# Own attention of the last block: values as the stationary operand, probabilities streaming, sums and inverses rearranged

## The reference, cut to what matters

```
def mha(xq, ctx, wq, wk, wv, wo, bo):
    ...
    scores = jnp.einsum('bhqd,bhkd->bhqk', q, k) / math.sqrt(DH)
    attn = jax.nn.softmax(scores, axis=-1)
    out = jnp.einsum('bhqk,bhkd->bhqd', attn, v)
    out = out.transpose(0, 2, 1, 3).reshape(b, sq, INNER)
    return out @ wo + bo
h1 = adaln(x, t, norm1_w, norm1_b)
x = mha(h1, h1, attn1_wq, ...) + x      # own attention: 256 queries, 256 keys
h2 = adaln(x, t, norm2_w, norm2_b)
x = mha(h2, context, attn2_wq, ...) + x # cross attention: 64 keys
h3 = adaln(x, t, norm3_w, norm3_b)
x = glu_ff(h3, ff_w1, ff_b1, ff_w2, ff_b2) + x
```

## Time and profile before

| | us |
|---|---|
| median of 3 runs | 5301.52 (5294.6 to 5302.85) |
| the profiled execution, its own time | 5300.39 |
| its span in the trace | 5298.2 |
| TensorE busy | 4622.3 (87% of the span) |
| VectorE / ScalarE / GpSimd busy | 2879.5 / 2086.8 / 574.2 |

### The profile page before, as it was taken

The page is one execution under the profiler, slowest core; times in us unless marked ns, Lnnn a source line. Parts: engine busy times, 40 slices in busy tenths (PEclk is TensorE's granted clock), DMA queues, the critical chain, the costliest instruction groups (busy, mean ns, idle before and its releaser), DMA issues. The chain is left out here.

```text
span 5298.2 us, 111277 instructions
## 1 busy us (share of the span) xinstructions
PE 4622.3 (87%) x45501; PEld 3101.2 (59%) x45501; DVE 2879.5 (54%) x9487; ACT 2086.8 (39%) x4096; POOL 574.2 (11%) x1298
## 2 busy tenths in 40 slices
PE   5489999999999974888898888998869898999884
PEld 3366777777777753555555555555434575766663
DVE  6734555555555542777766677666636423344433
ACT  2223333333333321566556666666623343222221
POOL 3301111111111112111111111111110000000000
PEclk8789999999999986999999999999979799899886
DMA  0010000000000012000000000000010001000000
GB/s 26 6 29 9 2 2 2 2 2 2 2 2 2 2 45 65 10 4 4 9 4 9 4 7 7 6 1 1 1 41 1 1 1 45 1 1 1 1 1 9
DMA packets 32703, 49.16 MB, mean 9 GB/s; under 512 B 8292, under 2 KB 23686, under 8 KB 31568
## 3 DMA queue, kind: packets, MB, share of 16 engines
q1 hardware_dynamic: 28880, 38.27, 2.3%
q10 hardware_dynamic: 2304, 2.11, 0.1%
q0 software_dynamic: 1024, 1.78, 0.1%
HBM read 37.72 MB, written 4.19 MB: 8 GB/s over the span
## 5 line engine op out<-in xcount | busy, mean ns | idle before, releaser
L2299 DVE TENSOR_REDUCE l_m<-psum 128x2 bf16<-128x512 f32 x768 | 504.0, 693 | 150.2 <-PE psum L1904 148.0
L1173 PE MATMUL psum<-g_still,ident_bf 128*128 128x256 bf16 (+3 forms) x1808 | 488.0, 295 | 1.5 <-PEq L58 1.5
L2175 ACT ACTIVATE l_probs<-psum,l_mcol 128x1024 f32<-128x1024 f32 x384 | 406.9, 1111 | 158.6 <-PE psum L1942 158.6
L1184 PE MATMUL psum<-g_gx,ident 128*128 128x128 f32 x1536 | 415.8, 389 | 0.0
L1904 PE MATMUL psum<-l_kb,l_qmb 32*128 32x256 bf16 x1536 | 295.5, 273 | 56.0 <-DVE l_m L2299 52.4
L1252 ACT ACTIVATE g_th<-g_pre 128x256 f32<-128x256 f32 x512 | 192.1, 419 | 314.3 <-DVE g_pre L1285 314.3
L1184 PEld LDWEIGHTS psum<-g_gx,ident 128*128 128x128 f32 x1536 | 279.3, 195 | 12.6
L2186 ACT COPY l_heads_out<-psum 128x256 f32<-128x256 f32 (+1 forms) x292 | 130.4, 446 | 371.4 <-PE psum L1968 188.4
L1942 PE MATMUL psum<-l_qm,l_keys 32*128 32x256 f32 x3072 | 264.7, 417 | 13.4 <-issue 13.4
L1285 DVE TENSOR_TENSOR g_pre<-g_encp,psum 128x256 f32<-128x256 f32 x512 | 192.8, 418 | 132.9 <-PE psum L1202 122.4
L2299 DVE TENSOR_REDUCE l_cm<-psum 128x4 bf16<-128x256 f32 x400 | 166.2, 428 | 179.8 <-PE psum L1904 179.6
(11 more groups left out here) (572 smaller groups left out, 9748.9 us busy)
## 6 DMA issues: line engine op xcount, KB each, us to landing
s_w<-in_S_w SPq DMA_DIRECT2D x16, 256.0 KB, 5.1
f_w<-in_F_w SPq DMA_DIRECT2D x2, 2048.0 KB, 12.3
l_wf<-in_L_W SPq DMA_DIRECT2D x6, 576.0 KB, 3.8
l_nw<-in_L_nw SPq DMA_DIRECT2D x1, 2304.0 KB, 8.1
l_wc<-in_L_W SPq DMA_DIRECT2D x6, 384.0 KB, 3.0
h_w<-in_H_W ACTq DMA_DIRECT2D x16, 129.0 KB, 3.1
h_w<-in_H_W SPq DMA_DIRECT2D x16, 129.0 KB, 3.1
l_wa<-in_L_W SPq DMA_DIRECT2D x6, 320.0 KB, 2.8
```

The lines of the kernel that those rows point to most:

```text
L1173: pe.matmul(psum[:, bank, 0:cols], cst["ident_bf"][:], still[:, 0:cols], start=True, stop=True)
L1184: pe.matmul(psum[:, bank, 0:P], cst["ident"][:], repeated(gx(gate, s)), start=True, stop=False)
L2175: act.activation(probs[:, u % 2, chunk, :].rearrange("p (g n) -> p g n", g=GROUP), psum[:, 0:GROUP, S * chunk:S * chunk + S], ACT.Exp, bia ...
L2299: dve.tensor_reduce(place, psum[:, c.bank(("max", u, g)), 0:x.tiles * x.width] .rearrange("p (t k) -> p t k", t=x.tiles), AX.X, ALU.min)\
```

## The change

`values(u, j)` now takes two of the four heads for all 256 queries: 64 columns of `v` are the stationary operand and the probabilities stream, one head into partitions 0 to 63, the other into 64 to 127 of bank 6 + j. The sums over the keys come from two more products of the same shape: the weights are 64 columns of ones, and `summed`, the two key halves of `probs` added by GpSimd, streams. So the sums lie beside the values, repeated on 64 partitions. ScalarE copies each bank (values and sums, 512 elements) to `values_sums`; VectorE's `own_normalise` inverts 256 elements and multiplies 256 into `qT`, feature-major. VectorE takes these between pairs of `row_max`. The transposes of `o` and their copies are gone from own attention: `self_project_out` is the products with `wo` alone. The column of ones is gone from `v`.

```diff
-                    def values(u, t):
+                    def values(u, j):
...
-                        g, b = divmod(u, 2)
-                        if t == 0:
+                        (g, b), n = divmod(u, 2), 2 * (base + u) + j
+                        if j == 0:
                             pe.wait_ge(sig["self_probs_ready"], 2 * (base + u + 1))
-                            if base + u >= 1:
-                                pe.wait_ge(sig["self_values_taken"], base + u)
                         elif u == 0 and p >= 1:
                             pe.wait_ge(sig["ff_taken"], p)
-                        for h in range(GROUP):
-                            for c in range(2):
-                                last = pe.matmul(psum[:, 6 + t, L3_COLS * h:L3_COLS * (h + 1)],
-                                                 probs[:, u % 2, c, 2 * (h % 2) + h // 2, P * t:P * t + P],
-                                                 v[:, 2 * b + c, GROUP * g + h, :], start=c == 0, stop=c == 1)
-                        if t == 1:
-                            last.then_inc(sig["self_values_ready"], 1)
+                        if n >= 2:
+                            pe.wait_ge(sig["self_values_copied"], n - 1)
+                        for c in range(2):
+                            for i, rows in enumerate(HALVES):
+                                pe.matmul(psum[rows, 6 + j, 0:S], v[:, 2 * b + c, GROUP * g + 2 * j + i, :],
+                                          probs[:, u % 2, c, 2 * i + j, :], start=c == 0, stop=c == 1)
+                        if j == 0:
+                            pe.wait_ge(sig["self_chunks_added"], base + u + 1)
+                        for i, rows in enumerate(HALVES):
+                            last = pe.matmul(psum[rows, 6 + j, S:2 * S], cst["ones"][:], summed[:, u % 2, 2 * i + j, :],
+                                             start=True, stop=True)
+                        last.then_inc(sig["self_values_ready"], 1)
...
+                def self_project_out(p):
+                    pe.wait_ge(sig["self_values_taken"], 2 * own_units * (p + 1))
+                    for ch in range(L3_CH):
+                        for t in range(PT):
+                            last = pe.matmul(psum[:, 4 + t, 0:D], qT[:, ch, P * t:P * t + P], wo[:, 0, ch, :],
+                                             start=ch == 0, stop=ch == L3_CH - 1)
+                    last.then_inc(sig["self_projected"], 1)
...
+                def chunks_added(at):
+                    pool.wait_ge(sig["self_probs_ready"], 2 * (at + 1))
+                    if at >= 2:
+                        pool.wait_ge(sig["self_values_ready"], 2 * (at - 1))
+                    pool.tensor_tensor(summed[:, at % 2, :, :], probs[:, at % 2, 0, :, :], probs[:, at % 2, 1, :, :], ALU.add)\
+                        .then_inc(sig["self_chunks_added"], 1)
...
+                def copy_values(at, j):
+                    n = 2 * at + j
+                    act.wait_ge(sig["self_values_ready"], n + 1)
+                    if n >= 2:
+                        act.wait_ge(sig["self_values_taken"], n - 1)
+                    act.copy(values_sums[:, j, :], psum[:, 6 + j, :]).then_inc(sig["self_values_copied"], 1)
...
-                    for u in range(own_units):
+                    for u in range(own_units + 1):
                         at = p * own_units + u
                         for c in range(2):
-                            exponentials("self", u, at, c, 1, 2 * c, 2 * at + c + 1)
-                    turned_out("self", p)
+                            if u < own_units:
+                                exponentials("self", u, at, c, 2, 2 * c, 2 * at + c + 1)
+                            if u >= 1:
+                                copy_values(at - 1, c)
...
+                def own_normalise(p, u, j):
+                    g, b = divmod(u, 2)
+                    n = 2 * (p * own_units + u) + j
+                    dve.wait_ge(sig["self_values_copied"], n + 1)
+                    dve.reciprocal(inverse[:, j, :], values_sums[:, j, S:2 * S]).then_inc(sig["self_sums_inverted"], 1)
+                    dve.wait_ge(sig["self_sums_inverted"], n + 1)
+                    dve.tensor_tensor(qT[:, 2 * g + j, S * b:S * b + S], values_sums[:, j, 0:S], inverse[:, j, :], ALU.mult)\
+                        .then_inc(sig["self_values_taken"], 1)
...
+                    for h in range(2):
+                        row_max("self", 1, base + 1, h, 2, S, m)
                     for u in range(own_units + 1):
-                        if u + 1 < own_units:
-                            for h in range(GROUP):
-                                row_max("self", u + 1, base + u + 1, h, 2, S, m)
-                        if u >= 1:
-                            g, b = divmod(u - 1, 2)
-                            normalise("self", base + u - 1, o[:, 2 * b:2 * b + 2, GROUP * g:GROUP * g + GROUP, :])
-                    turned_out("self", p)
+                        for j in range(2):
+                            ahead = u + 1 + j
+                            for h in ((2, 3) if j == 0 else (0, 1)):
+                                if ahead < own_units:
+                                    row_max("self", ahead, base + ahead, h, 2, S, m)
+                            if u >= 1:
+                                own_normalise(p, u - 1, j)
```

More of the change, by code:

```diff
@@ L3130, in glu_block @@
         qb, kb = sb("qb", [P, L3_CH, PTOK], BF16), sb("kb", [P, L3_CH, PTOK], BF16)
-        v, vc = sb("v", [P, PT, H, L3_COLS]), sb("vc", [P, H, L3_COLS])
+        v, vc = sb("v", [P, PT, H, L3_DH]), sb("vc", [P, H, L3_COLS])
         m = sb("m", [P, H * 4], BF16)
@@ L3136, in glu_block @@
         o = sb("o", [P, PT, H, L3_DH])
+        summed = sb("summed", [P, 2, GROUP, S])
+        values_sums, inverse = sb("values_sums", [P, 2, 2 * S]), sb("inverse", [P, 2, S])
         gT = o[:, 0:2, :, :].rearrange("p t h e -> p (t h e)").rearrange("p (f n) -> p f n", f=L3_FF)
@@ L3444, in _ @@
                         pe.wait_ge(sig["later_loads"], 112)
-                    project_out("self", 0, p, own_units * (p + 1))
+                    self_project_out(p)
                     cross_values_keys(p)
@@ L3469, in _ @@
                 for p in range(PAIRS):
+                    for u in range(own_units):
+                        chunks_added(p * own_units + u)
                     root("n2", p)
@@ L3609, in ff_added @@
                     dve.tensor_tensor(xall, xall, Y[:, p % 2, :, :], ALU.add)
-                dve.memset(v[:, :, :, L3_DH:L3_COLS], 1.0)
                 dve.memset(vc[:, :, L3_DH:L3_COLS], 1.0)
@@ L3634, in _ @@
                         dve.wait_ge(sig["v_ready"], 8 * p + j + 1)
-                        dve.tensor_copy(v[:, t, 8 * half:8 * half + 8, 0:L3_DH], heads(psum[:, v_bank(p, j), :]))\
+                        dve.tensor_copy(v[:, t, 8 * half:8 * half + 8, :], heads(psum[:, v_bank(p, j), :]))\
                             .then_inc(sig["v_taken"], 1)
```

## The result

The changed kernel takes 5253.85 us (median of 4 runs, 5246.44 to 5257.0); the kernel before, on the same chip, 5298.06 (4 runs, 5292.65 to 5302.85). The profiled execution took 5246.44 us with a span of 5244.6; it is the shortest of the four, so the two traces differ by more than the medians, 53.6 us of span.

A forecast was written before the change was run, and what follows sets the result against it. TensorE was taken to bound the kernel, with room on VectorE. Four pairs saving 6.3 in the body and 3.6 in the tail give 39.6 off 5300.4, 5260.8, so 5262 as median; eight-in-ten range 5247 to 5288 us.

The forecast's parts named there:

- The term of 6.3 a pair: Own attention before the tail: 13 values blocks a pair, each 0.48 us shorter, save 6.3 us a pair.
- The rival in which the halves exclude each other: Values block: output halves do not run side by side, 2.8 us instead of 1.45, kernel slower at 5334; chance 0.02.
- What is hidden: Own attention's half unit: VectorE's 3.55 us fits in 3.81, GpSimd's 2.35 us addition in about 3.6.
- The tail: From last scores to projection end: 19.7 us instead of 23.3, saving 3.6 a pair; bounds 16.7 and 24.5.
- the clock term: Tail: 10.2 us at half clock as before, making its end 19.7 us instead of 16.7 at full clock.
- The collisions: Own attention: VectorE's multiplication blocked by GpSimd's addition, six units losing 1 us, 5286; within VectorE falling behind, chance 0.14.
- The sum: Own attention and tail over four pairs: 4 x (6.3 + 3.6) = 39.6 us saved.
- the forecast's own range: Whole kernel: 5250 to 5274 us, for a tail of 16.7 to 22.7, chance 0.66.
- no change: Whole kernel: time as before, needing a projection wholly at half clock plus VectorE's collisions, 5299 or so; chance 0.06.

The follow-up runs named there:

- no inverse: The changed kernel without own attention's reciprocals, VectorE multiplying by the sums themselves: 5251.91 us, 0.9922 of the kernel before.
- addition twice: The changed kernel with a second GpSimd addition of the same size, into a spare tile, ahead of the one that counts: 5306.81 us, 1.0019 of the kernel before.

## Why the prediction was right, point by point

**TensorE's block and half unit.** 1.45 and 3.81 us, as predicted. The term of 6.3 a pair, 25.2 in all, was 22.7 in one pair of traces and 25.0 in the other; the difference is how long the clock is at half at the start of a body (58.3 to 62.2 us for the same instructions). So the two windows came out at 60.5 and 61.9, where near 59 and 61 was forecast: in pair 0 by PEclk some 7 us ran at half the clock, where before it were 4. The rival in which the halves exclude each other fell with the 1.45 and the 3.81.

**The durations that no row showed.** The reciprocal of 256 elements took 1.745 us against the 1.75 taken. The estimate from the Trainium skill (VectorE: DVE Perf Modes, "First, the fixed hardware budget"), 2.28 by a cycle for each of eight repeats, is contradicted by 64 instances here; the narrow reciprocals of the earlier trace rows gave the slope. Multiplication 0.425, copy 0.586, addition 2.352: as taken.

**What is hidden.** VectorE's chain per half unit was hidden (no inverse: the body does not move), and so was the addition, up to about 3.8 us (addition twice).

**The tail.** Its waits were forecast as 1.3 and 3.9 and are 1.24 and 3.85. Its clock was not: 10.2 us at half were assumed, as in the earlier trace rows, starting 4.2 us after the scores, behind the first idle time. The idle 1.24 us did not lower the clock here. It was still 1.00 up to 4530.5, and the fall came towards the end of the idle 3.85; the projection's own window is

```profile
4532.20:4541.20 9.00, 8.95 (x65) 8.97 (x66) 0.51 (x1) 0.00 (x0) 0.00 (x0) 0.82 0.01 2
```

At PEclk 0.91 over 18.3 us it was 3.3 us at half, and 6.9 in pair 2. At the full clock the tail would be 18.3 less half of 3.3, 16.6, and the prediction's figure for that case was 16.7. So the mechanism held and the clock term was too large, by about 1.1 us a pair: 18.6 instead of 19.7 as the prediction counts it.

**The collisions.** The rival priced them at 1 us a unit, 24 in all. The margin was thinner than forecast, 0.03 us instead of 0.3, and the blocking is real; the Trainium skill's rule (SBUF — State Buffer, "Who interferes with whom") agrees with both rows, 2.60 for the addition that came second and 1.03 for the multiplication that did. What a multiplication that comes second loses is about what is left of the addition. Started 1.6 us into it, that is 0.6 us (1.03 less 0.41), once in a unit: two halves of 3.5 us of VectorE's work (two maxima at 0.67, 1.745, 0.425) and 0.6 are 7.6 in a unit of 7.63, which still fits, and the body stayed as it was. Started early it would not fit: the 1.76 us lost by a start at 0.45 (2.17 less 0.41) would make 8.8 of 7.63, an estimated 1.1 us a unit, which is the rival's price. So the price stands, for an early start, which no run has in these units. What kept the collisions away is a margin of 0.03 us where 0.3 was forecast; that it was enough is in part luck.

**The sum.** Own attention with its tail saved 40.1 us in one pair of traces and 37.1 in the other, against 39.6. The whole span is more than that, 53.6 and 58.7 us, and holds three terms that the sum did not have: cross attention, where 10 and 6 us were lost to the clock; the phase ahead of the block, where 18.6 and 12.6 were gained; and all that comes before it, where 5.7 and 14.7 were gained. In the first two the traces of the two kernels don't overlap (240.9 and 246.3 against 251.1 and 252.2; 500.0 and 501.6 against 481.4 and 489.0); in the third the twelve traces with the change (3936.5 to 3957.8 us) lie on both sides of the two without (3950.6 and 3954.0), so it varies by execution. The medians fell by 44 and 39 us. So the sum is right for the stretch that it counts, and that the kernel's time came out within 8 us of the forecast is in part luck: the block alone gained 29 and 32, by which the time would have been about 5270, within the forecast's own range but at its upper end.

All twelve traces of kernels with the change show the phase ahead at 478.7 to 493.1 us, both traces without it at 500.0 and 501.6, with the same instructions. Most of the difference is in its first part, the attention: the same 1904 instructions of TensorE took 240.4 us at a clock of 0.83 in both traces before (3950.6 to 4191.0 in the first), and 223.6 at 0.91 and 231.0 at 0.87 in the two of the changed kernel. Why the clock there is better with the change is not settled; nothing that was tried bears on it. Nor is it settled why a kernel's cross attention falls into one pattern of the clock rather than another, or whether a delay of 1 us is enough to move it; that idle products take most of the time at half away is shown by one trace and by the time.

**A sum in the rivals.** For no change with the projection wholly at half the clock and VectorE's collisions on top, the prediction gives 5299. Its terms give more: a pair would save 6.3 - 6 and lose 1.2, so four are 3.6 us slower, 5305.

## What to carry to other kernels

When a matrix product is bound by its instructions, count what streams: 64 columns as the stationary operand, with the two halves of the output alternating, made 12 instructions of 16 and left the result in the layout that the next product needs, so that 32 transposes fell away. After such a change look at the tail first, where the longer chain stands open; starting the projection with the sample that is complete brought some 30 us (23 in the block) beside the change's own 39 to 44. And on a kernel with short waits don't judge an edit of a few us by the time alone: by the clock alone, stages that it doesn't touch moved by 5 to 20 us here, so compare the stage's own window, and only then ask whether the clock can be held.

## What the runs showed of the hardware that was not expected

- VectorE and GpSimd block each other in SBUF even where they start within 0.02 us of each other: 0.41 us for the first, 2.60 instead of 2.35 for the second. A multiplication started inside an addition, 0.45 to 1.6 us after its start, ends 0.27 to 0.29 us after it, less than its own 0.41; so it takes 2.17 to 1.03 us.
- A reciprocal of f32 costs 1.745 us for 256 elements per partition and 0.153 for one, so 0.0062 us for each further element.
- The granted clock of a stage with short waits differs from trace to trace, with the same code and partly with the same kernel: the same 461 instructions took 58.9 to 66.8 us (up to 69.6 with an extra reciprocal of 0.95 us ahead of them), and 57.0 with 120 idle products among them.
